# Local attention of a four-layer kernel, rebuilt on 64x64 quadrants with a per-tile order of work

## The reference, cut to what matters

```python
qkv = h @ wqkv[l]                       # 128 -> 3 x 512, as 8 heads of 64
q, k = l2norm(q) * q_scale[l], l2norm(k) * k_scale[l]
q, k = rotary_xpos(q, k)                # t * cos + rotate_half(t) * sin, with a scale per position
s = 8.0 * (q @ k.T)                     # 64 x 64 a sequence and head
s = where(causal, s, -inf)
o = softmax(s) @ v                      # 64 x 64 a sequence and head
x = x + merge_heads(o) @ wo[l]          # 512 -> 128
```

## Time and profile before

| | us |
|---|---|
| median of three runs | 3627.23 |
| lowest and highest | 3623.84, 3628.03 |
| the profiled execution | 3619.02 |
| its span | 3617.3 |
| `local_attention`, depth 0, in it (2042.8 to 2641.6) | 598.8 |
| `local_attention`, depth 1, in it (2815.6 to 3411.7) | 596.1 |

### The profile page before, as it was taken

The page is one execution under the profiler, slowest core; times in us unless marked ns, Lnnn a source line. Parts: engine busy times, 40 slices in busy tenths (PEclk is TensorE's granted clock), DMA queues, the critical chain, the costliest instruction groups (busy, mean ns, idle before and its releaser), DMA issues. The chain is left out here.

```text
span 3617.3 us, 87407 instructions
## 1 busy us (share of the span) xinstructions
PE 3215.5 (89%) x29616; PEld 2140.3 (59%) x29648; DVE 2596.8 (72%) x6356; ACT 1818.2 (50%) x3313; POOL 830.3 (23%) x1148
## 2 busy tenths in 40 slices
PE   4998769998999899988999499999989899999787
PEld 2665646665666566665666266666655566666445
DVE  5887868886777577765888577777756677777655
ACT  2665126563333255543666276767722567677522
POOL 1000000000000000001000366666611465666311
PEclk9999569998999899998999699999989999999999
DMA  4110001110000021100111100000001000000022
GB/s 136 30 29 16 0 10 30 29 26 1 0 0 0 16 42 39 39 7 11 30 28 26 53 9 7 8 7 7 4 21 26 13 6 9 6 9 6 13 70 58
DMA packets 193001, 79.14 MB, mean 22 GB/s; under 512 B 179125, under 2 KB 181865, under 8 KB 192233
## 3 DMA queue, kind: packets, MB, share of 16 engines
q1 hardware_dynamic: 191592, 73.25, 8.7%
q0 software_dynamic: 1280, 4.20, 0.3%
HBM read 35.58 MB, written 8.39 MB: 12 GB/s over the span
## 5 line engine op out<-in xcount | busy, mean ns | idle before, releaser
L770 ACT ACTIVATE probs_t<-ps_pt 128x1024 f32<-128x1024 f32 x256 | 262.0, 1023 | 384.9 <-PE ps_pt L884 384.9
L632 DVE TENSOR_REDUCE row_max<-ps_s 128x16 f32<-128x1024 f32 x256 | 313.0, 1223 | 132.4 <-PE ps_s L873 129.7
L1976 POOL TENSOR_TENSOR kblk<-kblk 128x512 f32<-128x512 f32 x256 | 325.5, 1271 | 209.7 <-DVE kblk L2019 209.7
L637 DVE TENSOR_TENSOR probs<-ps_s,row_max 128x1024 f32<-128x1024 f32 x256 | 311.8, 1218 | 11.7
L906 PE MATMUL ps_o<-v,probs_t 128*64 128x18 f32 x8192 | 285.1, 212 | 5.3 <-issue 5.2
L906 PEld LDWEIGHTS ps_o<-v,probs_t 128*64 128x64 f32 x8192 | 259.7, 138 | 40.2 <-issue 18.6
L884 PE MATMUL ps_pt<-ident,probs 128*128 128x128 f32 x2048 | 277.1, 278 | 3.9 <-ACT probs L765 3.9
L765 ACT ACTIVATE probs<-probs 128x1024 f32<-128x1024 f32 x256 | 269.5, 1053 | 16.4 <-DVE probs L637 15.0
L873 PE MATMUL ps_s<-kblk,q_t 64*64 64x512 f32 x2048 | 271.9, 604 | 6.6 <-issue 6.6
L616 POOL TENSOR_TENSOR x<-x,out_bias_L 128x512 f32 (+1 forms) x32 | 40.6, 1270 | 1025.2 <-DVE x_norm L426 517.9
L1991 POOL TENSOR_TENSOR kblk<-kblk,small_c 128x512 f32<-128x512 f32 x256 | 266.8, 1042 | 29.0 <-POOL small_c L1985 17.7
(11 more groups left out here) (313 smaller groups left out, 7027.0 us busy)
## 6 DMA issues: line engine op xcount, KB each, us to landing
ci<-in_ctx_t SPq DMA_DIRECT2D x64, 256.0 KB, 3.0
kblk<-k_t SPq DMA_DIRECT2D x768, 16.0 KB
ci<-x SPq DMA_DIRECT2D x64, 128.0 KB
ci<-x SPq DMA_DIRECT2D x128, 63.0 KB
x<-in_x_in SPq DMA_DIRECT2D x4, 1024.0 KB, 7.9
mask<-in_mask_l SPq DMA_DIRECT2D x64, 64.0 KB, 2.5
kblk<-ci SPq DMA_DIRECT2D x256, 16.0 KB
out<-x SPq DMA_DIRECT2D x1, 4096.0 KB, 11.2
```

Of the source, the lines that this page charges most:

```text
L632: dve.tensor_reduce(row_max[u % 2][:, :], scores_of(u), AX, ALU.max).then_inc(max_ready.sem, 1)
L637: dve.tensor_tensor(probs[u % 2][:, :, :], scores_of(u), row_max[u % 2][:, :].unsqueeze(2).broadcast_to([P, HEADS, S]), ALU.subtract).then ...
L770: act.activation(probs_t[:, :, :], ps_pt[:, :, :].rearrange("p a (r t) -> p (a r) t", t=P), ACT.Copy).then_inc(pt_ready.sem, 1)
L1976: pool.tensor_tensor(a, a, b_, ALU.add).then_inc(rotated.sem, 1)
```

## The change: scores on quadrants, one signal a tile, division ahead of the transposition

- Wide operations: squares, the straight product of the rotation, the addition and the scaling on POOL, and the copy of turned q and k take both q and k, 1024 elements in one instruction. The crossed products are two of 512 for both, in place of four of 256. v and its copy are one of 512.
- No padding: a head pair's second head lies on partitions 64 to 127, as the transposition leaves it. `scores` runs 16 matmuls of 64 rows, 64 columns of weights and 64 of data, two heads by two sequences on the four quadrants, behind four mask matmuls of 256 columns. `project_v` writes v with the pair's heads on the two halves of the partitions. `weigh_values` has v as weights and the turned probabilities as data, 16 matmuls of 64x64x64, rows and columns on the same half, and so gives the output already turned: `turn_o` and its bank are gone.
- The division goes to POOL and ahead of `turn_probs`: `scale_probs` multiplies the 512 probabilities by the reciprocals. `divide` is gone.
- PSUM: turned q and k and the scores share two banks; v and the turned probabilities have one each, the latter shared with the window's transpositions.
- Order: q and k are projected three tiles ahead, all four engines run by `run_pipeline` with a reach of one group, and each waits tile by tile.
- The three clearings in `prepare_layers` are gone; the tables are waited for by DVE, not by PE.

The diff, cut to the new side of what the prediction speaks of:

```diff
                     def project_v(g, t, par):
+                        wait_tile(pe, v_copied, g, t - 1)
...
+                        for b in range(2):
+                            for j in range(2):
+                                last = pe.matmul(bank_v[j * S:(j + 1) * S, b * 2 * P:(b + 1) * 2 * P],
+                                                 h[:, b * S:(b + 1) * S], w_v[:, :, j, :], start=True, stop=True)
                     def turn_qk(g, t):
+                        wait_tile(pe, unit, g, t)
+                        wait_tile(pe, qk_copied, g, t - 1)
+                        wait_tile(pe, shifted, g, t - 1)
...
                     def scores(g, t):
+                        wait_tile(pe, qk_copied, g, t)
...
+                        for j in range(2):
+                            rows = slice(j * S, (j + 1) * S)
+                            for b in range(2):
+                                pe.matmul(bank_ts[b * S:(b + 1) * S, j, 0:2 * P], ident_16[rows, rows],
+                                          masks["causal"][rows, :].unsqueeze(1).broadcast_to([S, LPAIRS, S]),
+                                          start=True, stop=False, skip_group_check=True)
                         for r in range(LPAIRS):
+                            for j in range(2):
+                                rows = slice(j * S, (j + 1) * S)
+                                for b in range(2):
+                                    tok = slice(r * P + b * S, r * P + (b + 1) * S)
+                                    last = pe.matmul(bank_ts[b * S:(b + 1) * S, j, r * S:(r + 1) * S],
+                                                     qk_t[rows, 0, tok], qk_t[rows, 1, tok],
+                                                     start=False, stop=True, skip_group_check=True)
                     def turn_probs(g, t):
+                        if t == 1:
+                            wait_past(pe, xt_ready, g + 1, 1 if has(g + 1) else 0)
+                        wait_tile(pe, p_scaled, g, t)
+                        wait_tile(pe, pt_copied, g, t - 1)
...
                     def weigh_values(g, t):
...
+                                for j in range(2):
+                                    rows = slice(j * S, (j + 1) * S)
+                                    at = t % 2 * INNER + b * 2 * P + r * LD
+                                    last = pe.matmul(ps_o[rows, tok], v_rows[rows, at:at + LD], pt[rows, tok],
+                                                     start=True, stop=True)
                     # PE, for each u in range(GT); every call only where the tile exists
+                            project_qk(g, u + 3, par)
+                            weigh_values(g, u)
+                            if u == 0 and has(g + 1):
+                                transpose_window(g + 1, 1 - par)
+                            project_v(g, u + 2, par)
+                            turn_qk(g, u + 2)
+                            project_o(g, u)
+                            turn_probs(g, u + 1)
+                            scores(g, u + 2)
                     # ACT
+                            copy_qk(g, u + 1)
+                            copy_pt(g, u)
+                            roots(g, u + 2)
+                            copy_v(g, u + 1)
+                            if u == 0 and has(g + 1):
+                                copy_window(g + 1, 1 - par)
+                            exponentials(g, u + 1)
+                            squares(g, u + 3)
+                            copy_ot(g, u)
                     # POOL
+                    def scale_probs(g, t):
+                        wait_tile(pool, rec_ready, g, t)
...
+                        pool.tensor_tensor(p3, p3, inverse.unsqueeze(2).broadcast_to([P, LHEADS, S]), ALU.mult)\
+                            .then_inc(p_scaled.sem, 1)
...
+                            normalise_qk(g, u + 1)
+                            scale_probs(g, u)
+                            unite(g, u + 2)
                     # DVE
+                            sums(g, u + 1)
+                            rotate(g, u + 3)
+                            cross(g, u + 3, 1)
+                            cross(g, u + 3, 0)
+                            sum_squares(g, u + 3)
+                            maxima(g, u + 2)
+                            residual(g, u)
```

More of the change, by code:

```diff
@@ L1808, in scores, with project_qk @@
[L1808 to L1813, removed]
+                    def project_qk(g, t, par):
+                        if t % GT == 0:
+                            pe.wait_ge(xt_ready.sem, xt_ready.at(g + t // GT, 1))
+                        wait_tile(pe, products, g, t - 1)
+                        wait_tile(pe, squared, g, t - 1)
+                        pe.matmul(bank_qk[:, 0, :], tokens(t, par), w_qkv[l][:, 0:INNER], start=True, stop=True)
+                        pe.matmul(bank_qk[:, 1, :], tokens(t, par), w_qkv[l][:, INNER:2 * INNER],
+                                  start=True, stop=True).then_inc(qk_in_psum.sem, 1)
@@ L1822, in turn_probs @@
[L1822 to L1834, removed]
-                                last = pe.matmul(ps_o[b * S:(b + 1) * S, r * P:(r + 1) * P],
-                                                 pt[:, r * P + b * S:r * P + (b + 1) * S],
-                                                 v_pair[u % 2][:, b, r, :, :].rearrange("p j d -> p (j d)"),
-                                                 start=True, stop=True)
-                        last.then_inc(summed.sem, 1)
@@ L1841, in turn_o @@
-                    def turn_o(g, u):
-                        pe.wait_ge(o_ready.sem, o_ready.at(g, u + 1))
-                        for r in range(LPAIRS):
-                            last = pe.transpose(bank_t[:, r * P:(r + 1) * P], o_[:, r * P:(r + 1) * P], ident[:, :])
-                        last.then_inc(ot_in_psum.sem, 1)
-                    def project_o(g, u):
-                        pe.wait_ge(ot_copied.sem, ot_copied.at(g, u + 1))
-                        pe.wait_ge(added.sem, added.at(g, u))
+                                tok = slice(r * P + b * S, r * P + (b + 1) * S)
@@ L1886, in _, with copy_window @@
                     act.preload_act_table_set(LN_EXP)
[L1888 removed]
+                    def copy_window(g, par):
                         act.wait_ge(xt_in_psum.sem, xt_in_psum.at(g, 1))
[L1890 to L1897 removed]
@@ L1956, in body @@
                                 roots(g, u + 2)
[L1957 to L1968 removed]
+                            if next_:
+                                copy_v(g, u + 1)
```

414 lines of the change are left out of this document (177 added, 237 removed).

## The result

| | us |
|---|---|
| before, 4 runs beside it | 3625.53 (3619.01 to 3628.03) |
| after, 4 runs | 3566.81 (3561.60 to 3568.55) |
| ratio, 95% interval | 0.9838 [0.9821, 0.9855] |
| profiled execution, after | 3568.55 (span 3566.9) |
| predicted | 3506 (3425 to 3585) |

A forecast was written before the change was run, and what follows sets the result against it. A ring through the engines, no engine alone, was taken to bound the kernel. Two stages 118 us and memsets 3 off 3619.0 gave 3498 profiled, 3506 with the 8.2 distance kept; 80% range 3425 to 3585.

The forecast's parts named there:

- The ring: In local attention, a chain through the engines from a tile to the tile after next: 14.9 us undisturbed, 17.4 slow.
- the walk: Four tiles followed, each instruction starting at the later of its operands and its engine: 32.3 us, 8.08 a tile.
- an undisturbed ring: Two tiles through the engines of local attention with nothing else in the way: 7.4 us a tile.
- PE's sum of 7.1: PE's own work for one local-attention tile after the change: 7.1 us, against 8.1 before.
- The window's term: Once in four tiles, the exponential stands behind `copy_window` on ACT and starts 2.5 us late.
- Rival (a): The window costs nothing, slack swallows the late exponential: 7.4 to 7.6 us a tile, about 3430 us; chance 0.22.
- The sizes: Durations taken for a tile's new operations: addition 2.4 us, scaling 1.95, scores 0.6, masks 0.2, weighing 1.1.
- Rival (b): A tile's sizes are the upper ones, with longer hops: 8.6 to 8.8 us a tile, about 3570 us; chance 0.20.
- rival (c): TensorE loses its clock in local attention: a third at 1.2 GHz gives 3740 us, all 4200; chance 0.08.
- clip 0.2: In the sum of DVE's work for a tile, 6.5 us, the clip counted as 0.2 us.
- Memsets: Three memsets before the tables fall away, 0.91 us each in DVE's order: 3 us.
- The ends: From the last scores to a stage's end, 9.0 us for 10.3: 1.3 less in each stage.

The follow-up runs named there:

- experiment 2: Changed kernel with the clip moved from DVE to ACT as a scaled copy, without its lower bound: 3491.24 us, ratio 0.9643 to before.
- experiments 5 to 7: Changed kernel with window's copy behind exponential and squares, plus: clip on ACT 3438.03 us; POOL's addition in halves 3437.72; sums of squares in PSUM 3455.63.
- (4): Changed kernel with only ACT's order altered, the window's copy behind exponential and squares: 3508.67 us, ratio 0.9683 to before.
- experiments 1 to 3: Changed kernel with the clip reading PSUM 3532.17 us; with the clip on ACT 3491.24; with POOL's addition in two halves 3507.85.

## Why the prediction was half right

- **The ring, and that no engine alone holds the tile: right for the changed kernel.** With the lock out of the way and the window left in its place four tiles take 31.9 (experiment 2), where the walk has 32.3, and the four intervals are the walk's to within 0.6. That experiments 5 to 7 have the 7.4 forecast for an undisturbed ring shows less: PE is busy 98% there and its own work is 7.2 a tile, so either would give that time, and the agreement is in part luck. PE's sum of 7.1 was right to 0.1.
- **The window's term: right.** 2.5 us late was forecast, 2.19 measured, 2.2 for four tiles when taken away (4), where the walk's 32.3 less four times 7.4 is 2.6. Rival (a) was wrong for the reason given against it.
- **The sizes: right.** Addition 2.36 (2.4), scaling 1.90 (1.95), division of probabilities 1.05 (1.05), scores 0.56 (0.6), masks 0.13 (0.2), weighing 1.08 (1.1). Rival (b) named nearly the measured time, 3570, for reasons that did not happen.
- **Clock, rival (c): not as named, but 3 us of it.** The stages are at 0.99 of full, the level of 2.4 GHz, but for the microseconds behind the stall and the three short stretches at 0.50 in stage 2; the kernel before has 1.00 in both stages.
- **The step that failed: "clip 0.2".** In DVE's sum the clip is 0.2, and in the ring it does not appear: the small steps follow straight on the addition, as if the roots were ready by then, and the maxima straight on the scores. Both take each engine's durations as its own. The clip takes 1.32 whenever POOL's addition is in flight, which by the new order is in every tile. That puts 0.7 between scores and maxima (2303.10 to 2303.81) and 0.7 between addition and small steps (2303.86 to 2304.57), 1.4 in a ring of two tiles: 0.7 a tile by this sum. Taken away, the lock is worth 2.0 to 2.1 in four tiles, 0.5 a tile (experiments 1 to 3). The walk was 0.4 too long without it (32.3 for 31.9), so that over the group 1.7 are missing, 34.0 for 32.3: 53 of the 70 us by which the profiled execution (3568.55) misses 3498, by the intervals of both stages.
- **Not in the prediction at all: the stall.** One of 7 us; with the 3 us of the clock, 10. PE's code had grown (34384 matmul records for 29616), and the prediction counted instructions as time on the engine, not as bytes to bring.
- **Memsets.** They are gone, 3 us, but in this execution the cross attention ahead of them ended 3.5 us later, so that the first exponential is at 2068.8 for 2068.6, 3 us later than forecast.
- **The ends.** Behind the last exponentials of the two stages 1.3 us less each were forecast; 0.3 less and 2.4 more were measured, 5 us in all. 53, 10, 3 and 5 make the 70, but for rounding. The second tile's scores follow the first's after 9.0 us and not 5.6, but the last group, which has no window to wait for, makes up for it.
- **The distance of 8.2** between the profiled execution and the median, kept from the kernel before, is -1.7 in the changed one. That chance took 10 of the 70 us off again: the median misses 3506 by 61.

The Trainium skill has the lock (SBUF — State Buffer, "SBUF: two separate sides"): of VectorE in a mode that uses both ports and GpSimd, whichever starts first keeps the shared pair of SBUF ports for its whole instruction. VectorE: DVE Perf Modes ("What auto-detection actually checks") puts into such a mode an operation whose single source and destination are in SBUF, with sizes that are even or equal, as the clip's 16 are. The runs agree in each point: the clip with an SBUF source waits for the end of POOL's addition, with a PSUM source it takes 175 ns, and the straight product, which reads PSUM beside SBUF, lies beside POOL's scaling at its usual 1.23. But the reduction L2017, SBUF to SBUF, overlaps the addition's start and neither is longer for it, and the reciprocal L2040 takes its 0.20 in the middle of POOL's scaling. In the kernel before the reciprocal lies in the middle of POOL's addition 124 times and takes the same 0.20. So not all that have source and destination in SBUF are held, and it isn't what POOL runs that spares them: of the kinds compared here only that of the clip, `tensor_scalar`, is held.

The trace of before could have told. There the clip takes 174, 175 and 329 ns (least, median, most), and the two long ones, 313 and 329, are those that met POOL's scaling:

```profile
L2030 DVE TENSOR_SCALAR small_a<-small_d x128: 174/175/329, 2055.3 to 3393.3; 128x16 f32<-128x16 f32 x128
...
2060.09 1.04 POOL L1991 TENSOR_TENSOR kblk<-kblk,small_c 128x512 f32<-128x512 f32 x1
2060.83 0.33 DVE L2030 TENSOR_SCALAR small_a<-small_d 128x16 f32<-128x16 f32 x1
```

It ends 0.03 after the scaling. And an earlier stage has one `tensor_scalar` of 128x128 (L426) that started beside a POOL multiplication of 1.04 us (L1562) and took 1049 ns for the usual 340. The question was whether the new order would bring clip and POOL together in every tile.

## What to carry to other kernels

When an order changes, look in the trace of before for small VectorE instructions whose longest duration is far above the median, and at what GpSimd ran beside that one. Then list which VectorE instructions with source and destination in SBUF (element by element with a scalar, as the clip) will now fall beside a GpSimd operation, however small they are: one of 16 numbers is held for up to the length of POOL's. Give the small one a PSUM source, another engine, or a gap by splitting POOL's. And when a term is taken off a ring of several engines, check what covers it: here the scores could get 0.3 us slower at no cost to three intervals of four, because the lock was last.

## What had not been expected of the hardware

- The clip, 128x16 SBUF to SBUF: 1321 ns in the median beside POOL's addition of 2357, 175 in the median outside it, and 175 from PSUM in the midst of it.
- 32 records of 64x64x64: 0.56 us with the four quadrants in turn, 0.85 with the row half outermost, 1.08 for the weighing on the diagonal two.
- A PE loop of nine packets of 16 KB is brought again at some passes: 4.4 to 5.2 us without work, then matmuls at half pace (granted clock 0.50) for some 5 us (2248.58 to 2253.8 in the changed kernel), 5.9 to 7.8 us in all each time.
